# Calls of the first blocks stand elsewhere in the lists of all engines, in a fused attention and feed-forward kernel

## What is computed

```python
q, k, v = x @ Wq, x @ Wk, x @ Wv               # 16 heads of width 8
fg = sigmoid(x @ Wf + bf)
# over time, for each head, an 8 x 8 state:
state = state * g[..., None] + v[..., None] * k[..., None, :]
out_t = einsum('bhij,bhj->bhi', state, q)
# then
out = layernorm(out) * gamma + beta
out = (out * silu(x @ Wg)) @ Wout
x = layernorm(x + out)
h = silu(tlin(x, w1)) * tlin(x, w2)            # tlin: product with ternary weights, times a scale
h = gelu(tlin(h, h1)); h = gelu(tlin(h, h2))   # 512 wide
x = layernorm(x + tlin(h, w3))
```

## Time and profile before

| | |
|---|---|
| time, median of 3 runs | 509.78 us (507.11, 509.78, 509.82) |
| span of the profiled execution | 505.3 us |
| TensorE busy | 495.5 us, 98% |
| VectorE busy | 447.2 us, 89% |
| ScalarE busy | 405.6 us, 80% |
| GpSimd busy | 310.0 us, 61% |
| granted TensorE clock | 1.000 |

### The profile page before, as it was taken

The page is one execution under the profiler, slowest core; times in us unless marked ns, Lnnn a source line. Parts: engine busy times, 40 slices in busy tenths (PEclk is TensorE's granted clock), DMA queues, the critical chain, the costliest instruction groups (busy, mean ns, idle before and its releaser), DMA issues.

```text
span 505.3 us, 8095 instructions
## 1 busy us (share of the span) xinstructions
PE 495.5 (98%) x2528; PEld 383.7 (76%) x2528; DVE 447.2 (89%) x708; ACT 405.6 (80%) x839; POOL 310.0 (61%) x362
## 2 busy tenths in 40 slices
PE   8999999999999999999999999999999999999997
PEld 6667787877878787777877777787777778687896
DVE  4999899999999999999999999899999999994171
ACT  5677788887897877879798787989878797978955
POOL 0842839577392948748394875748486584928423
PEclk9999999999999999999999999999999999999999
DMA  7999989718079976698897790880797592520001
GB/s 257 226 252 240 208 215 221 194 48 205 0 187 227 244 180 134 155 219 197 190 237 180 178 236 3 189 208 1 169 225 168 138 210 71 121 67 1 22 3 65
DMA packets 43372, 79.47 MB, mean 157 GB/s; under 512 B 4928, under 2 KB 5952, under 8 KB 43072
## 3 DMA queue, kind: packets, MB, share of 16 engines
q1 hardware_dynamic: 43040, 78.61, 63.7%
q10 hardware_dynamic: 288, 0.33, 0.2%
HBM read 11.81 MB, written 4.19 MB: 32 GB/s over the span
## 4 chain that ended last, share of the span: by engine, by line
PE 69%; DVE 9%; issue 8%; POOL 8%; ACT 3%; SPq 2%; DMA 1%; POOLq 0%; ACTq 0%; DVEq 0%
PE F L2301 41%; PE back L2402 8%; PE front L2202 6%; DVE KJ L1557 4%; PE back L2287 2%; POOL h1lo L441 2%; PE back L2186 2%; PE ps_v L2202 2%; POOL h2lo L441 2%; PE back L2269 2%; SPq L283 2%; POOL KJ L502 1%; PE F L2198 1%; DMA QJ<-qk 1%; DVE h L1621 1%
## 5 line engine op out<-in xcount | busy, mean ns | idle before, releaser
L441 POOL TENSOR_TENSOR h1lo<-h,h1hi 128x512 fp32r<-128x512 f32 x60 | 76.4, 1290 | 18.5 <-ACT h1hi L864 18.2
L871 ACT ACTIVATE h<-F,cols 128x512 f32<-128x512 f32 x120 | 80.5, 686 | 8.6 <-PE F L2301 7.6
L441 POOL TENSOR_TENSOR h2lo<-h,h2hi 128x512 fp32r<-128x512 f32 x60 | 76.1, 1290 | 10.6 <-ACT h2hi L864 10.4
L1557 DVE TENSOR_TENSOR_SCAN KJ<-g,carry,KJ 128x512 f32<-128x512 f32 x64 | 78.3, 1264 | 0.3 <-ACT g L803 0.2
L1557 DVE TENSOR_TENSOR_SCAN KJ<-g,KJ 128x512 f32<-128x512 f32 x64 | 74.3, 1203 | 0.4 <-ACT g L803 0.3
L508 POOL TENSOR_TENSOR QJ<-QJ 128x512 f32<-128x512 f32 x14 | 18.0, 1283 | 91.6 <-DVE QJ L1572 91.6
L2301 PE MATMUL F<-h2hi,whi 128*128 128x512 f32 (+1 forms) x256 | 72.1, 417 | 0.7 <-ACT h L871 0.5
L1564 DVE TENSOR_TENSOR QJ<-QJ,KJ 128x1024 f32<-128x1024 f32 x60 | 71.4, 1213 | 1.0 <-DMA QJ<-qk 0.8
L2301 PE MATMUL F<-h1hi,whi 128*128 128x512 f32 (+1 forms) x256 | 70.7, 414 | 1.0 <-DVE h L1621 0.8
L2301 PE MATMUL F<-h1lo,whi 128*128 128x512 f32 (+1 forms) x256 | 67.7, 401 | 0.2 <-POOL h1lo L441 0.2
L2301 PE MATMUL F<-h2lo,whi 128*128 128x512 f32 (+1 forms) x256 | 66.4, 402 | 0.0
(11 more groups left out here) (182 smaller groups left out, 937.9 us busy)
## 6 DMA issues: line engine op xcount, KB each, us to landing
KJ<-qk SPq DMA_DIRECT2D x120, 256.0 KB, 4.8
QJ<-qk SPq DMA_DIRECT2D x120, 256.0 KB, 4.8
x_in<-in_x SPq DMA_DIRECT2D x16, 256.0 KB, 4.7
xT<-in_xT SPq DMA_DIRECT2D x15, 256.0 KB, 5.0
out<-res SPq DMA_DIRECT2D x15, 256.0 KB, 2.0
wraw<-in_wffn SPq DMA_DIRECT2D x2, 1024.0 KB, 8.8
wraw<-in_wffn SPq DMA_DIRECT2D x2, 256.0 KB, 4.7
wproj<-in_wproj SPq DMA_DIRECT2D x2, 192.0 KB, 3.7
```

The lines of the kernel that those rows point to most:

```text
L441: e.tensor_tensor(h_lo[layer][:, t, :w], h[:, t, :w], h_hi[layer][:, t, :w].bitcast(f32), ALU.subtract).then_inc(lo_done[layer], 1)
L871: e.activation(dst[:, t, :WIDTH[n]], F[t][:, :WIDTH[n]], ACT.Gelu, scale=scale[t]).then_inc(gelu_done[layer], 1)
L1557: e.tensor_tensor_scan(K, g[:, :WIDTH[n]], K, init, ALU.mult, ALU.add).then_inc(scan_done, 1)
```

## The change

No instruction is added to or taken from the computation. Calls change places in the five lists, all in blocks 0 to 3. In `fetch` the waits that guarded the first half of a block's transfers now guard both halves. The wait for the first projection weights moves from the main list into `project` for block 0. The diff, cut:

```diff
 def fetch(n, which, half):
-                if half == 0:
-                    if which and n == 2:
...
+                if which and n == 2:
...
 # SP
+            load_xT(2)
+            load_xT(3)
+            load_w3()
             load_weights(0)
+            load_x(0)
+            fetch(1, 1, 0)
+            fetch(1, 1, 1)
             load_weights(1)
             load_weights(2)
...
+            load_weights(3)
             fetch(1, 0, 0)
...
             fetch(1, 0, 1)
+            fetch(2, 1, 0)
+            fetch(2, 1, 1)
             load_xT(4)
...
 # GpSimd
             kvj_gp(2)
+            qsj_gp(1)
             kvj_gp(4)
-            qsj_gp(1)
             kvj_gp(6)
             qsj_gp(2)
-            scale_w3()
             qsj_gp(3)
+            rstd_of(0, "o")
             kv_gp(1, 4)
             kv_gp(1, 5)
-            rstd_of(0, "o")
...
             rstd_of(1, "o")
+            scale_w3()
...
 # ScalarE
+            hi_0(0)
+            copy_v(0)
             halve_bias()
-            hi_0(0)
             hi_0(1)
-            copy_v(0)
...
             copy_v(2)
+            sum_low_parts(1)
+            sum_low_parts(2)
             sum_low_parts(3)
             norm_1(0)
+            split_weights(1)
             x1_hi(0)
+            split_weights(2)
             silu_gate(2)
             silu(0, 0)
             silu(0, 1)
...
+            split_weights(3)
...
 # VectorE
+            lo_0(0)
             make_selectors()
-            lo_0(0)
             lo_0(1)
...
             residual_1(0)
-            qs(1, 0)
             stats_1(0)
...
             find_low_parts()
-            qs(1, 1)
+            qs(1, 0)
+            scan(1, 7)
             set_flag()
             x1_lo(0)
-            scan(1, 7)
+            qs(1, 1)
...
-            kv(2, 0)
             hmul(0, 2)
             hmul(0, 3)
             stats_o(1)
+            kv(2, 0)
             kv(2, 1)
...
 # TensorE
+                if n == 0:
+                    e.wait_ge(wproj_landed[0], 16)
...
                 up_hi(0, 0, low_parts)
+                up_lo(0, 0, low_parts)
                 up_hi(0, 1, low_parts)
-                up_lo(0, 0, low_parts)
...
-                last_begin(0)
                 up_hi(1, 0, low_parts)
                 up_lo(1, 0, low_parts)
+                last_begin(0)
                 last_rest(0)
...
             project_0(0)
+            project_v(0)
             project_0(1)
-            project_v(0)
+            project_f(0)
             project_kj(0)
...
             keep_busy(16, F[3])
+            keep_busy(1, F[3])
             transpose_x1(0)
             count_low_parts()
-            keep_busy(1, F[3])
```

More of the change, by code:

```diff
@@ L268, in fetch @@
             def fetch(n, which, half):
-                if half == 0:
-                    if which and n == 2:
[L271 to L278, removed]
+                if which and n == 2:
+                    e.wait_ge(qsj_done, len(QS_VECTOR))
+                    e.wait_ge(qsj_gp_done, len(QS_GP))
+                    e.wait_ge(carry_done, 1)
+                elif which and n > 2:
+                    e.wait_ge(qs_done, NPAIR * (n - 2))
+                    e.wait_ge(carry_done, n - 1)
+                elif n > 1 and not which:
+                    e.wait_ge(oT_made, n - 1)
                 e.wait_ge((q_copied, k_copied)[which], n)
@@ L548, in _ @@
             add_gp(2)
+            lo(1, 1, 0)
             kv_gp(3, 6)
-            kv_gp(3, 7)
-            lo(1, 1, 0)
             rstd_of(2, "o")
@@ L556, in _ @@
             gated_y(2)
-            rstd_2(0)
+            kv_gp(3, 7)
             lo(2, 1, 0)
@@ L562, in _ @@
             lo(2, 1, 3)
+            rstd_2(0)
             kv_gp(4, 6)
@@ L997, in _ @@
             silu(0, 1)
-            split_weights(3)
[L999 to L1007, removed]
+            copy_q(3)
+            save_carry(1)
+            hi(1, 0, 0)
+            hi(1, 0, 1)
+            silu(0, 2)
+            silu(0, 3)
+            g_of_tanh(2)
+            hi(1, 0, 2)
+            hi(1, 0, 3)
+            split_weights(3)
             norm_o(1)
@@ L1020, in _ @@
             norm_1(1)
-            copy_v(3)
+            gelu(2, 0, 0)
+            gelu(2, 0, 1)
             copy_q(4)
             x1_hi(1)
-            gelu(2, 0, 0)
-            g_of_tanh(3)
-            gelu(2, 0, 1)
+            save_carry(2)
             gelu(2, 0, 2)
+            copy_v(3)
             gelu(2, 0, 3)
-            save_carry(2)
             silu(1, 0)
@@ L1032, in _ @@
             silu(1, 1)
-            square(0)
+            g_of_tanh(3)
             silu_gate(3)
@@ L1038, in _ @@
             hi(1, 1, 2)
+            norm_o(2)
             hi(1, 1, 3)
-            norm_o(2)
             affine(2)
@@ L1050, in _ @@
             hi(2, 1, 3)
+            square(0)
             norm_1(2)
@@ L1694, in _ @@
             scan(0, 0)
+            scan(0, 1)
             kvj(3)
-            scan(0, 1)
+            scan(0, 2)
             kvj(5)
-            scan(0, 2)
             scan(0, 3)
+            scan(0, 4)
             kvj(7)
-            scan(0, 4)
             scan(0, 5)
@@ L2488, in rest @@
                 up_lo(1, 1, low_parts)
+                project_gate(3)
+                sum_transposed(2)
                 up_hi(1, 2, low_parts)
-                sum_transposed(2)
-                project_gate(3)
                 up_lo(1, 2, low_parts)
@@ L3140, in _ @@
             project_qj(7)
+            project_f(3)
             sum_j(6)
-            project_f(3)
             sum_j(7)
             project_gate(0)
+            project_gate(1)
             keep_busy(4, back)
-            project_gate(1)
+            project_k(3)
             keep_busy(1, back)
+            transpose_y(0)
             project_v(2)
-            project_k(3)
-            transpose_y(0)
             project_q(2)
```

55 lines of the change are left out of this document (20 added, 35 removed).

## The result

The changed kernel takes 512.52 us in the median of 7 runs (509.3 to 513.5) against 507.72 (507.04 to 509.82) for the kernel before in 7 runs. The ratio, before and after compared round by round, is 1.0060, 95% interval 1.0039 to 1.0080: **slower by about 0.6%**. The forecast said 1.1 us, which is inside 0.5%. The range held the time; the likeliest case, a loss of 0.4 to 2 us, did not come true. In every run whose span is on record the time lies 1.8 to 1.9 us above that run's own span, so the slower runs of a kernel are executions whose span was longer, and not equal ones with more around them.

What follows compares the result with a forecast made beforehand. TensorE (98% busy) and VectorE (89%) were taken as the bound, so moves cost only where TensorE waits. Up to the branch 0.05 plus block 1's 1.05 made 1.1 us on 509.78: 510.9 us, range 507.6 to 513.2.

Steps and rivals of the forecast that it cites:

- the likeliest case: Whole kernel: a loss of 0.4 to 2 us, time likeliest 510.9 us, chance 0.53.
- the sum: Whole span: 505.3 + 0.05 + 1.05 = 506.4 us, a loss of 1.1 us.
- the first 20 us: Head of VectorE's list: idle about 1 us before the third scan, `qsj(4)` 0.3 us later, passed on to `attention_out(0)`.
- with 0.5 us to spare: ScalarE before the branch: sums put `norm_1(0)` at 40.0 to 40.9 us, inside the 41.45 of `transpose_x1(0)`.
- the load at 0.49 us: Branch at 42 us: TensorE loads the flag in 0.49 us, first product 1.30 us after the cast's start, at 43.8.
- each queue it is moved past: Transfers: 5.25 MB up to q's first half land at 33.4 us, asked for at 40.2, 6.8 us to spare.
- the order of `up_lo(0, 0)`: Behind the branch on TensorE: `up_lo(0, 0)` behind `up_hi(0, 0)` takes back the 0.4 us delay, leaving 0.0 to 0.1.
- `split_weights(3)` and `scale_w3` are covered: Moved into waits of 3.00 us on ScalarE and 1.86 us on GpSimd; both were to cost nothing.
- block 1: VectorE's list makes `x1_lo(1)` 2.26 us later, near 72.6; TensorE waits 1.05 us, bounds 0 to 1.5.
- Nothing gives it back: Behind block 2: lists are equal, all engines about 1 us late alike, so the loss stays.
- Rival 2: Weights in q's way: `qs(1, 0)` waits for q below 183 GB/s, 516 us at 155; slower side together 0.19.
- Rivals 1 and 3: 1: loss absorbed, 509.5 to 510.0 us, chance 0.15; 3: later blocks give something back, 506 to 507, chance 0.13.

Runs made afterwards that it cites:

- a_gp: Changed kernel with `rstd_of(0, "o")` put back behind `kv_gp(1, 4)` and `kv_gp(1, 5)` on GpSimd; 509.51 us.
- a_quiet: Changed kernel with SP holding back the second half of block 2's k transfers until TensorE's first up product behind the branch; 510.71 us.
- b_up: Kernel before with only `up_lo(0, 0)` moved right behind `up_hi(0, 0)` on TensorE; 508.80 us.
- b_dve1: Kernel before with only VectorE's list of block 1 changed, `kv(2, 0)` behind `stats_o(1)` and `qs(2, 2)` ahead of `x1_lo(1)`; 510.25 us.
- a_dve1: Changed kernel with VectorE's list of block 1 put back as before; 511.09 us.
- a_four: Changed kernel with `rstd_of(0, "o")`, the flag ahead of `scan(1, 7)`, VectorE's block 1 list and held-back k transfers edited together; 510.76 us, ratio 1.0059.
- b_sp: Kernel before with only SP's transfers in the changed kernel's order, up to `fetch(3, 1, 0)`; 509.13 us.
- a_again: Changed kernel, unchanged, run and traced once more; 512.29 us.
- a_warm: Changed kernel with six more `keep_busy` products behind `project_gate(2)`, filling TensorE's wait for the flag; 511.31 us, ratio 1.0074.
- b_best: Kernel before with `up_lo(0, 0)` behind `up_hi(0, 0)`, `qs(1, 0)` behind the statistics, `split_weights(2)` behind `x1_hi(0)`, `keep_busy` 11 for 16; 508.07 us, ratio 1.0004.

## Why the prediction was right or wrong

**The range held partly by luck.** It was laid around 509.78 us, the median of three runs of before; the median of seven is 507.72. Laid from there at the same distances it would end at 511.1 us, and 512.52 lies above. By the medians the loss is 4.8 us and by the ratio 3.0 us, where the sum had 1.1.

**Right: the first 20 us.** VectorE's wait before the third scan was 0.86 us (about 1), and from `kvj(0)` to `qsj(4)` it took 11.02 us (11.05 by the forecast, 11.36 before). The 0.3 us that were to be left at `attention_out(0)` came out as 0.08 (34.03, 33.95) in one pair of traces and 0.18 (34.66, 34.48) in the other, where two executions of before differ by 0.53.

**Wrong: "with 0.5 us to spare" for ScalarE's sums.** I compared their end, 40.0 us, with `transpose_x1(0)` at 41.45, and that held: TensorE waited 0.20 us there. But the same sums feed `find_low_parts`, which VectorE reaches at 40.07 us, and they ended at 40.6. `copy_v(2)` came 0.3 us later than I had it, and a sum behind a sum costs 2.10 us from start to start (36.49 to 38.59), not 1.9. So the cast came 0.84 us later from att0. The sum had 0.4 from the start of the program, and 0.3 of that was the shift of att0, so 0.1 in these terms. `a_gp` shows 0.65 of it to be the place of `rstd_of(0, "o")`.

**Wrong: the load at 0.49 us.** The earlier trace rows is one instruction in one state of SP's queue. The change moves eight fetches into that moment, and the load took 0.82 and 1.32 us; `a_quiet` shows 0.486 with SP silent. The step "each queue it is moved past" was made for the landing of q only. It is the term of +0.30 to +0.81, from the cast to the first product.

**Right: the order of `up_lo(0, 0)`** gives 0.46 us back (`b_up`). It was to pay for all of the flag's delay, 0.4 us, and pays for 0.46 of 1.15 to 1.65. Right too: `split_weights(3)` and `scale_w3` are covered (the waits ahead of `norm_o(1)` and of the gate's product at 61.03 us shrink from 3.00 to 2.36 and from 1.86 to 0.62, and both come later by no more than TensorE does).

**Right in mechanism, mis-sized: block 1.** VectorE's wait before `stats_o(1)` is 1.79 us (2.3), and from there to `x1_lo(1)` it takes 20.26 us, 2.24 more than before (2.26). TensorE's wait for `x1lo` is 0.58, not 1.05, as TensorE itself arrives late, with 0.47 of new wait for GpSimd's `h2lo`, behind the `rstd_of(1, "1")` that `qs(2, 0)` held up: together 1.05 again. The stretch as a whole lost 1.28 us, inside the bounds of 0 to 1.5. `b_dve1` measured the list by itself at 2.04 in the kernel before, where nothing covers a part of it; `a_dve1` at 0.55 in the kernel after, because `x1_hi(1)` is late too. I had named that as a bound and priced it at 0.45 us; with VectorE's list as before, 0.73 (`a_dve1`) and 0.76 (`a_four`) are lost all the same.

**"Nothing gives it back" was right; that nothing more is lost is open.** The tail is +0.90 and +0.39 in the two pairs, within the spread of all kernels, and VectorE waits in block 13 for a transfer of q in both, 0.81 us before and 1.41 after:

```profile
389.99 1.22 DVE L1564 TENSOR_TENSOR QJ<-QJ,KJ 128x1024 f32<-128x1024 f32 x1 [0.81 <-DMA QJ<-qk]
```

```profile
393.50 1.22 DVE L1563 TENSOR_TENSOR QJ<-QJ,KJ 128x1024 f32<-128x1024 f32 x1 [1.41 <-DMA QJ<-qk]
```

**The rivals.** Rival 2 had the side right. Its mechanism, `qs(1, 0)` waiting for q, did not come in after: q landed at 36.3 us, 2.9 later than the 33.4 of the forecast, and was asked for at 40.70. It did come in `b_sp`, 1.40 us long, where `qs(1, 0)` stands in its old place. In after transfers did harm through the load of the flag. Rivals 1 and 3 did not come. The sum, 1.1 us, should have been: 0.84 + (0.30 to 0.81) - 0.46 + 1.28, which is 2.0 to 2.5 us to the middle layer of block 1; the measured ratio is 2.0 to 4.1 us.

**What stays open:** the 1.77 us at the end of the span, which only `after`, `a_again` and `a_warm` have of the kernels traced (in the eleven others the last store lands 1.83 to 1.85 us behind the start of VectorE's last instruction, in these three 3.52 to 3.62); why `a_four` is as slow as after by its ratio; by what the load is lengthened, beyond the run of slow issues that its long cases share; and what the many moves cost or gain that no run took apart, those of ScalarE and TensorE above all.

## What to carry to other kernels

For each moved call list every reader of what it feeds, and compare its new end with the earliest of them, not with the one on the chain of waits. Where the lists are dense, price a moved call both at the place it leaves and at the place it goes to: time ahead of a wait is free, and here `kv(2, 0)` and `qs(1, 0)`, which left such time, came back as waits of the next hand-over. A move that gains nothing by itself can still cover what another costs: `qs(1, 0)` behind the statistics hides the later landing of q. Look also at what a moved call will run beside: `qs(2, 0)` held up an instruction of GpSimd from 0.2 to 1.2 us. And undo a part in the kernel after as well as making it alone in the kernel before: 0.55 against 2.04 us for one edit says that a second cause lies beneath it.

## What the runs showed of the hardware

- A load of one word from SBUF into TensorE's register took 0.486 to 0.492 us in seven traces and 0.640, 0.687, 0.820, 0.993, 1.089, 1.268 and 1.324 us in the seven where SP had issued eight fetches in the 11 to 12 us before without a rest and was issuing still. Issuing after a rest into engines at a share of 1.02 to 1.09 left it at 0.488 (`b_best`).
- A GpSimd TENSOR_TENSOR of 128x4 took 1.14 to 1.18 us when VectorE ran a 128x1024 TENSOR_TENSOR (`qs`) at the same time, in seven traces of seven, and 0.19 to 0.24 beside VectorE's scans, its `hmul` and its `kv`, which reads one input from `ps_v`.
- TensorE's clock fell to the lower level behind a wait of 1.71 us in one execution (0.57 over the next 3 us) and stayed at 1.00 behind one of 1.75 us in another.
- On ScalarE a sum that accumulates starts 0.19 us after the recorded end of the sum before it, the reading of the accumulator (0.19 us) lying between; an instruction without an accumulator starts some 0.1 us before the recorded end of the one ahead.
- From the start of VectorE's last instruction to the end of the span it took 2.27 to 2.32 us in eleven traces and 4.04 to 4.07 in three, with the last store landing as much later.
